# Silu on ScalarE, the last layer's batch 0 first, and the third attention's additions dealt out: a two-layer transformer of 2 x 128 tokens on one core

## The chip, the cores and the metric

The kernel runs on one core of one Trainium2 chip, in one launch. The metric is the device time of that launch in microseconds (us). The engines are PE (TensorE), DVE (VectorE), ACT (ScalarE), POOL (GpSimd) and SP, which issues most DMAs; each takes its own instructions in order and waits for the others by semaphores.

## What the reference computes

Six residual blocks run one after the other over `x`, 2 batches of 128 tokens by 128 channels, each on a layer norm of `x`:

```python
x = x + cross_attention(ln(x), ctx)        # A: causal, so only the first tile of the context counts
x = x + self_attention_with_rope(ln(x))    # B: causal
x = x + top2_of_8_experts(ln(x))           # C: routing, capacity 20, relu MLP
x = x + masked_cross_attention(ln(x), ctx, mask)   # D
x = x + gated_scan(ln(x))                  # E
x = x + bitlinear_mlp(ln(x))               # F
```

What the change touches, cut to what matters:

```python
probs = softmax(x @ Wr + br); topk_p, topk_e = top_k(probs, 2)             # C
scores = where(keep, scores, -inf); out = softmax(scores) @ v              # D
u = silu(conv(u)); b, c = split(u @ W_bc + b_bc)                           # E
state = state * a + b;  y = state * c * sigmoid(gate);  y @ W_out + b_out  # E
gate = silu(bitlinear(x, w_gate)); up = bitlinear(x, w_up)                 # F
return bitlinear(gate * up, w_down)      # F: rounds its input with a scale from each row's greatest |value|
```

## The kernel before, in words

Tokens lie on the 128 partitions, and the two batches are separate tiles. The order of the work is written out by hand: one program for each engine, with semaphores between them, so that an instruction that waits holds up all that stands behind it on its engine. PSUM's eight banks have fixed uses: `S` is banks 0 to 3, `T` 4 and 5, `O` 6 and `D` 7, and `bank(half, g)` is the same memory seen by halves. `keep_warm(name)` (L1036) is a row of `WARM[name]` PE products of constants that nobody reads. A float32 product on PE is two passes in the trace (x2 for one `mm`).

**C, routing** (L1256 to L1281 on PE, L753 to L798 on DVE). PE makes the logits and adds their bias `br` with a product of one row (K=1). DVE takes the greatest, ACT the exponential, and DVE goes through a chain of small operations: the top 2, one-hot rows (`oh1`, `ohb`, `oh`), the softmax's sum and quotient (`lsum`, `lmax`, `prob`, `gates`), and from PE's count of earlier tokens the places and the dispatch matrix `disp` (L790). PE gathers the tokens with it (`C_buf`), ACT copies both batches to `buf` (L452), PE turns the combine matrix `comb` (L1279) and starts the experts' first layer (L1285, four groups `i`). In code `link` makes DVE wait for the end of an instruction; instructions without it follow each other closely.

**D, the third attention** (PE from L1415, DVE from L910, ACT L492). Two context tiles per batch and 16 heads make four *pairs* q = 0 to 3 (two for each batch), each of four banks i. For each pair PE puts the mask's bias and the scores into four banks, DVE takes the maxima (`greatest_of_pair`, R), joins and scales them (RJ, MQ, EX), PE turns RJ between (`turn_maxima_of_pair`) and subtracts EX from the scores (`subtract_of_pair`), ACT takes the exponential of one bank after the other into PX (L495), and PE adds up (`add_up(q, i)`: 8 products, 4 for the sums and 4 for the weighted values, 16 passes in the trace). Both pairs of a batch add to one region (`sums_and_outputs`), which a product sets to zero first. DVE then divides (`divided_by_sums`, RC and AT), PE projects (`project_pairs`), and DVE adds to X and starts the next layer norm. Pair 2 takes its scores into the banks that pair 0 left, pair 3 those of pair 1, except its bank 0.

**E, the scan** (PE from L1478, DVE from L935, ACT L502). PE makes u and the gate from xnT with `win`; half 1 of u's convolution runs on PE (`taps`, 4 products), half 0 on DVE (`conv`, L938 to L945). ACT takes tanh(u/2) (L507, L509) and DVE makes `su` = u (1 + tanh(u/2)), which is 2 silu(u) (L949). PE makes b and c from su (16 passes), DVE adds b's bias and halves it (`bT`, L957), scans (L961), applies the gate (L966) and c with its bias (L971), and PE makes the output (`wout`), whose bias row is multiplied by 4 (`fours`, L1505).

**F, the last layer** (PE from L1515, DVE from L987, ACT L517). For each batch DVE rounds the normed tokens to integers (xq), PE turns them, ACT copies them (xqT) and PE makes gate and up. PE turns both batches before the first gate product (L1516 to L1523). ACT takes the tanh (L523), and DVE makes the product in two instructions (L1006, L1008), the greatest of each row and the scale (L1010 to L1012). ACT scales and rounds both batches (L526), DVE finishes both (hq, L1015), PE turns hq and multiplies with the down weights, and DVE adds to X (L1022), which SP stores.

The core of F on DVE before:

```python
for b in range(B):
    e.wait_ge(sem("F_th"), b + 1)
    link(e.scalar_tensor_tensor(hm[:, b, :], thf[:, b, :], 1.0, S[:, 2 * b, :], ALU.add, ALU.mult))        # L1006
    link(e.scalar_tensor_tensor(hm[:, b, :], hm[:, b, :], kk[:, b:b + 1], S[:, 2 * b + 1, :], ...))        # L1008
    link(e.tensor_reduce(hmax[:, b:b + 1], hm[:, b, :], AX.X, ALU.max, apply_absolute_value=True))         # L1010
    ...
```

Of the kernel before, what the change touches and what calls it, by code (L numbers as in the profile page):

```python
# [13 lines left out]
P = 128  # L14
B = 2
# [12 lines left out]
WARM = dict(A_greatest=5, A_second=4, C_route=9, C_place=3, F_wait=18, B_keys=3, B_queries=3, C_first=2, C_second=3, C_third=0, D_greatest=8, D_second=3,  start=17, A_q=4, A_norm=4, B_norm=7, C_norm=7, D_norm=5, E_conv=4, E_gate=2, E_norm=9)  # L28
# [20 lines left out]
ROWS, ROWS_W = columns(bv=P, bo=P, br=E, bproj=P, bout=P, cb=P)  # L49
# [6 lines left out]
def program(nc, d):  # L56
    with ExitStack() as ctx:
# [51 lines left out]
        fours = sb("fours", [1, P])  # L109
# [98 lines left out]
        th = sb("th", [P, 2, B * P])  # L208
# [3 lines left out]
        bT = sb("bT", [P, 2, B * P])  # L212
# [4 lines left out]
        bbc2 = sb("bbc2", [P, 2])  # L217
# [43 lines left out]
        def pair_bank(q, i):  # L261

            return bank(0, 0) if q == 3 and i == 0 else bank(q % 2, i)

        def spare_of(q):

            return (bank(1, 0)[:, 0:P], bank(0, 0)[:, 0:P], bank(1, 1)[:, 0:P], bank(1, 0)[:, 2 * P:3 * P])[q]

        def sums_and_outputs(b):

            region = (bank(1, 0), bank(0, 1))[b]
            return region[:, 0:P], region[:, P:2 * P]
# [50 lines left out]
        def _(e):  # L323
            e.memset(neghalf[:, :], -0.5).then_inc(sem("pool_const"), 1)
            e.memset(ones[:, :], 1.0).then_inc(sem("pool_const"), 1)
            e.memset(fours[:, :], 4.0).then_inc(sem("pool_const"), 1)
# [34 lines left out]
            e.tensor_scalar(bbc2[:, :], part(scanw, SCAN, "bbc")[:, 2:4], 2.0, None, ALU.mult).then_inc(sem("scan_const"), 1)  # L361
# [25 lines left out]
        def _(e):  # L387
# [62 lines left out]
            for b in range(B):  # L450
                e.wait_ge(sem("C_buf"), b + 1)
                e.activation(buf[:, :, b, :], T[:, b, 0:E * SLOTS].rearrange("p (e s) -> p e s", e=E),  # L452
                             ACT.Copy).then_inc(sem("C_bufs"), 1)
# [38 lines left out]
            for q in range(2 * B):  # L492
                for i in range(G):
                    e.wait_ge(sem("pair_shifted"), G * q + i + 1)
# [12 lines left out]
            e.activation(th[:, 1, :], O[:, 0:B * P], ACT.Tanh, scale=0.5).then_inc(sem("E_th"), 1)  # L507
            e.wait_ge(sem("E_conv"), 1)
            e.activation(th[:, 0, :], conv[:, :, :].rearrange("p b t -> p (b t)"), ACT.Tanh,  # L509
                         scale=0.5).then_inc(sem("E_th"), 1)  # L510
# [9 lines left out]
            for b in range(B):  # L520
# [1110 lines left out]
```

## Time and profile before

| what | value |
|---|---|
| time, median of 3 runs | 142.76 us (142.53 to 145.39) |
| time of the profiled execution | 142.53 us |
| its span, first to last instruction | 140.40 us |
| around the span | 2.13 us |
| busy: PE, DVE, ACT, POOL | 118.4, 85.7, 38.3, 31.5 us |
| chain that ended last | PE 64%, DVE 25%, ACT 6%, issue 3%, POOL 1% |
| mean granted PE clock | 0.979 of full speed |

The times in the rows are microseconds from the span's start, so a row's start plus its length can be set against the next row's start. The chain of waits is followed back from the last instruction: a piece in it ended last among what the next piece waited for. A busy PE isn't a PE on that chain, since the keep-warm products count as busy. The ends of products are modelled: in a row of passes the distance between starts is the cost of one, and the last one's length comes on top.

### The profile page before, as it was taken

Reading aid. Unit: us, or ns where it says so; the run is one execution under the profiler, and the core shown is the slowest. Engines: PE = TensorE matmul, PEld = TensorE weight load, DVE = VectorE, ACT = ScalarE, POOL = GpSimd, SP = SyncE. Lnnn points to the kernel's source line nnn. Section 1 sums busy time; section 2 is a strip of 40 time slices with the busy share of each in tenths; the row PEclk is TensorE's granted clock in tenths of the full one; section 3 lists DMA queues with packets and bytes.
Section 4 is the critical chain, followed back from the end, with each engine's and each line's share of the span. In section 5 each row is a group of like instructions: output and inputs, shape, how many; then the busy total and the mean of one; then the engine's idle time right before and its main releaser. Section 6 shows DMA issues by size and latency. Waiting matters only on the chain.

```text
span 140.4 us, 2885 instructions
## 1 busy us (share of the span) xinstructions
PE 118.4 (84%) x1189; PEld 70.1 (50%) x1189; DVE 85.7 (61%) x227; ACT 38.3 (27%) x88; POOL 31.5 (22%) x53
## 2 busy tenths in 40 slices
PE   6999776986798699789999998789997989983932
PEld 2464223761425365459995542355475467741411
DVE  0635867666958354595325578575746425977872
ACT  3140052400141522137330300551414034002340
POOL 8930000011000011000001199999401100030000
PEclk9999999999999999999999999999999779999996
DMA  3989993010000000000000000000000000000001
GB/s 131 375 296 424 430 421 138 25 51 9 0 0 5 0 0 0 5 0 0 0 5 0 0 7 0 0 0 5 0 7 5 0 5 0 0 0 0 2 0 37
DMA packets 3225, 8.35 MB, mean 60 GB/s; under 512 B 357, under 2 KB 1673, under 8 KB 2954
## 3 DMA queue, kind: packets, MB, share of 16 engines
q1 hardware_dynamic: 3066, 7.72, 14.4%
q10 hardware_dynamic: 144, 0.43, 0.9%
q8 instruction: 10, 0.16, 0.5%
q14 instruction: 5, 0.04, 0.1%
HBM read 8.02 MB, written 0.13 MB: 58 GB/s over the span
## 4 chain that ended last, share of the span: by engine, by line
PE 64%; DVE 25%; ACT 6%; issue 3%; POOL 1%; DVEq 0%; POOLq 0%
PE banks L1029 35%; DVE R L581 5%; PE banks L1403 5%; PE banks L1046 3%; PE banks L1373 3%; PE banks L1061 3%; ACT PX L495 3%; PE banks L1305 3%; PE banks L1387 3%; DVE R L882 2%; PE banks L1069 2%; PE banks L1079 2%; PE banks L1034 1%; PE banks L1365 1%; ACT PX L397 1%
## 5 line engine op out<-in xcount | busy, mean ns | idle before, releaser
L1029 PE MATMUL banks<-onesb 128*128 128x512 bf16 x123 | 32.5, 403 | 2.7 <-POOL onesb L327 1.3
L344 POOL TENSOR_TENSOR rstd<-veps,neghalf 128x1 f32<-128x1 f32 x12 | 6.6, 552 | 91.1 <-DVE veps L563 91.1
L1029 PEld LDWEIGHTS banks<-onesb 128*128 128x128 bf16 x123 | 11.7, 102 | 18.6 <-issue 6.5
L397 ACT ACTIVATE PX<-banks 128x512 f32<-128x512 f32 x16 | 8.3, 603 | 18.6 <-PE banks L1046 18.6
L495 ACT ACTIVATE PX<-banks 128x512 f32<-128x512 f32 x16 | 8.3, 602 | 17.8 <-PE banks L1387 17.8
L581 DVE TRANSPOSE_TENSOR_REDUCE R<-banks 128x32 f32<-128x1024 f32 x8 | 9.5, 1227 | 3.6 <-PE banks L1061 3.6
L882 DVE TRANSPOSE_TENSOR_REDUCE R<-banks 128x64 f32<-128x2048 f32 (+2 forms) x6 | 9.5, 1597 | 3.2 <-PE banks L1373 3.2
L412 ACT ACTIVATE xnT<-banks 128x128 f32<-128x128 f32 x10 | 2.7, 280 | 20.5 <-PE banks L1034 20.5
L1029 PE MATMUL banks<-buf,w 128*128 128x64 f32 x64 | 7.3, 276 | 0.0
L1029 PEld LDWEIGHTS banks<-buf,w 128*128 128x128 f32 x64 | 7.2, 192 | 0.1
L568 DVE TENSOR_SCALAR xn<-X,mv,rstd 128x128 f32<-128x128 f32 x12 | 4.1, 344 | 4.8 <-POOL rstd L344 4.8
L1403 PE MATMUL banks<-PX,oneg 128*32 128x128 f32 x128 | 6.6, 279 | 0.0
L557 DVE TENSOR_TENSOR X<-X,banks 128x128 f32<-128x128 f32 x8 | 2.3, 286 | 7.1 <-PE banks L1029 7.1
L561 DVE BATCH_NORM_STATS2 stats<-X 128x6 f32<-128x128 f32 x12 | 3.5, 294 | 4.8 <-DMA X<-in_x 4.4
L1403 PE MATMUL banks<-PX,VX 128*32 128x128 f32 x128 | 6.4, 273 | 0.0
L1373 PE MATMUL banks<-QS,KT 32*128 32x512 f32 x32 | 6.2, 587 | 0.0
L1046 PE MATMUL banks<-EX,ones 32*128 32x512 f32 x32 | 5.0, 636 | 1.2 <-DVE EX L591 1.1
L1029 PE MATMUL banks<-constb 128*128 128x512 bf16 x16 | 4.8, 382 | 1.4 <-DVE QT L713 0.9
L1069 PE MATMUL banks<-PX,oneg 128*32 128x128 f32 x128 | 4.9, 278 | 1.2 <-ACT PX L397 1.2
L373 POOL TENSOR_SCALAR wtmp<-wtmp 128x512 f32<-128x512 f32 x3 | 5.8, 1935 | 0.3
L1061 PE MATMUL banks<-QB,KT 32*128 32x512 f32 x32 | 5.4, 630 | 0.3 <-DVE QB L574 0.3
L1387 PE MATMUL banks<-EX,ones 32*128 32x512 f32 x32 | 5.2, 613 | 0.0
(222 smaller groups left out, 206.9 us busy)
## 6 DMA issues: line engine op xcount, KB each, us to landing
w<-in_w SPq DMA_DIRECT2D x4, 512.0 KB, 7.5
w<-in_w SPq DMA_DIRECT2D x2, 1024.0 KB, 11.5
scanw<-in_scanw SPq DMA_DIRECT2D x1, 906.0 KB, 13.8
ffn<-in_ffn SPq DMA_DIRECT2D x1, 768.0 KB, 15.0
const<-in_const ACTq DMA_DIRECT2D x1, 417.5 KB, 3.5
selfw<-in_selfw SPq DMA_DIRECT2D x1, 384.0 KB, 3.7
first<-in_first SPq DMA_DIRECT2D x1, 321.0 KB, 4.2
cross<-in_cross SPq DMA_DIRECT2D x1, 320.0 KB, 4.1
```

Source lines behind the costliest of these rows:

```text
L344: e.tensor_tensor(rstd[:, b:b + 1], veps[:, b:b + 1], neghalf[:, 0:1], ALU.pow).then_inc(sem("rstd"), 1)
L397: e.activation(PX[:, u, g, :], bank(half, g), ACT.Exp).then_inc(sem(f"ex{u}"), 1)
L495: e.activation(PX[:, q, i, :], pair_bank(q, i), ACT.Exp).then_inc(sem("pair_exp"), 1)
L581: e.tensor_reduce(R[:, b, 2 * k:2 * k + 2, 0:J * G], banks[:, 4 * b + 2 * k:4 * b + 2 * k + 2, :].rearrange("p g (c i) -> p g c i", i=32), ...
L882: step(e.tensor_reduce(R[:, q % 2, first:first + n, 0:J * G], source.rearrange("p g (c i) -> p g c i", i=32), AX.X, ALU.max, negate=True, ...
L1029: return e.matmul(out, lhsT, rhs, start=start, stop=stop, skip_group_check=True)
L1046: e.matmul(bank(half, g), quarter(ones, g)[:, :], quarter(EX, g)[:, b, :, :].rearrange("p j k -> p (j k)"), start=False, stop=True, tile_p ...
L1061: e.matmul(bank(b, g), quarter(KT, g)[:, b, :], quarter(QB, g)[:, b, :, :].rearrange("p j k -> p (j k)"), start=False, stop=False, tile_po ...
L1069: last = e.matmul(bank(b, 1)[32 * j:32 * j + 32, 0:P], oneg[:, 32 * g:32 * g + 32], PX[:, b, g, j * P:(j + 1) * P], start=(g == 0), stop=( ...
L1373: e.matmul(pair_bank(q, i), quarter(KT, i)[:, q, :], quarter(QS, i)[:, q, :, :].rearrange("p j k -> p (j k)"), start=False, stop=False, ti ...
L1387: e.matmul(pair_bank(q, i), quarter(ones, i)[:, :], quarter(EX, i)[:, q % 2, :, :].rearrange("p j k -> p (j k)"), start=False, stop=True, ...
L1403: last = e.matmul(region[32 * j:32 * j + 32, :], w, PX[:, q, i, j * P:(j + 1) * P], start=False, stop=end, tile_position=(0, 32 * j), skip ...
```

## The change

It does the following (of PE's part of D the diff shows the calls without their waits):

- **Routing (C)**: both bias products of the logits stand ahead of the two batches' products. The softmax's sum, reciprocal, quotient and gates move from among the one-hot operations to behind the dispatch. Batch 1's `buf` is copied by DVE. PE turns `comb` after the first group of the experts' first layer.
- **Third attention (D)**: the additions stand one at a time where PE waited, in the order below. Pair 2 too takes its bank 0 apart (its maximum in two instructions), bank 0 of pairs 2 and 3 comes last in subtraction, exponential and addition, the sums have other banks, and the zeroing is one bf16 product. The row `D_second` (3) goes, `D_divide` (3, ahead of the last projection) comes, `D_norm` is 7 for 5. DVE normalises batch 0 (L926) after batch 1's division.
- **Scan (E)**: ACT takes Silu in place of Tanh, with one Silu of a single column after the last exponential. DVE's `su` and `bT` operations go; b's bias comes by four K=1 products on PE, ahead of `E_conv`, which is 1 for 4. The gate keeps its Tanh.
- **Last layer (F)**: PE turns batch 0 and makes its gate and up products before it turns batch 1. ACT takes Silu, DVE's product is one instruction; ACT rounds batch 0, DVE batch 1. `F_wait` is 12 for 18.

```diff
-WARM = dict(... F_wait=18, ... D_greatest=8, D_second=3, ... D_norm=5, E_conv=4, ...)
+WARM = dict(... F_wait=12, ... D_greatest=8, ... D_norm=7, D_divide=3, E_conv=1, ...)
...
         def pair_bank(q, i):
-            return bank(0, 0) if q == 3 and i == 0 else bank(q % 2, i)
+            if i == 0 and q > 1:
+                return (bank(1, 0), bank(0, 1))[q - 2]
+            return bank(q % 2, i)
+        def unit_order(q):
+            return (0, 1, 2, 3) if q < 2 else (1, 2, 3, 0)
...
# ACT
+            e.activation(tabled[:, :], part(scanw, SCAN, "ld")[:, 0:1], ACT.Silu)
...
-            e.activation(th[:, 1, :], O[:, 0:B * P], ACT.Tanh, scale=0.5).then_inc(sem("E_th"), 1)
+            e.activation(su[:, 1, :], O[:, 0:B * P], ACT.Silu).then_inc(sem("E_su"), 1)
...
                 e.activation(tile(xqT, b), T[:, b, :].bitcast(BF16)[:, 0:P], ACT.Copy).then_inc(sem("F_xqs"), 1)
-            for b in range(B):
                 e.wait_ge(sem("F_gate"), 2 * b + 1)
                 e.wait_ge(sem("F_ch"), b + 1)
-                e.activation(thf[:, b, :], S[:, 2 * b, :], ACT.Tanh, scale=ch[:, b:b + 1]).then_inc(sem("F_th"), 1)
+                e.activation(thf[:, b, :], S[:, 2 * b, :], ACT.Silu, scale=ch[:, b:b + 1]).then_inc(sem("F_th"), 1)
...
# DVE, routing: after disp
+            link(e.tensor_reduce(lsum[:, :], lg[:, :, :], AX.X, ALU.add))
+            link(e.reciprocal(lmax[:, :], lsum[:, :]))
+            e.wait_ge(sem("C_buf"), 2)
+            e.tensor_copy(buf[:, :, 1, :], T[:, 1, 0:E * SLOTS].rearrange("p (e s) -> p e s", e=E)).then_inc(sem("C_bufs"), 1)
+            link(e.tensor_tensor(prob[:, :, :], lg[:, :, :], lmax[:, :].unsqueeze(2).to_broadcast([P, B, E]), ALU.mult))
+            link(e.tensor_tensor(gates[:, :, :], oh[:, :, :], prob[:, :, :], ALU.mult))
...
# DVE, third attention
-            greatest_of_pair(2, 12, 0, 4)
+            greatest_of_pair(2, 11, 1, 3)
+            greatest_of_pair(2, 12, 0, 1)
...
             first_batch("D_")
-            normalise(4, 0)
             divided_by_sums(1)
...
+            normalise(4, 0)
             residual("D_", 1)
...
# DVE, last layer
-            link(e.tensor_tensor(kk[:, :], ch[:, :], fx[:, :], ALU.mult))
-            link(e.tensor_scalar(kk[:, :], kk[:, :], wmean[:, 1:2], None, ALU.mult))
+            link(e.tensor_scalar(kk[:, :], fx[:, :], wmean[:, 1:2], None, ALU.mult))
+            def product(b):
+                e.wait_ge(sem("F_th"), b + 1)
+                e.wait_ge(sem("F_gate"), 2 * b + 2)
+                link(e.scalar_tensor_tensor(hm[:, b, :], thf[:, b, :], kk[:, b:b + 1], S[:, 2 * b + 1, :], ALU.mult, ALU.mult))
+            def rounded(b):
+                e.tensor_scalar(hq[:, b, :], thf[:, b, :], MAGIC, 127.0, ALU.subtract, ALU.min).then_inc(sem("F_hq"), 1)
+            product(0)
+            peak(hm[:, 0, :], hmax[:, 0:1], kd[:, 0:1], sh[:, 0:1], "F_sh")
+            product(1)
+            e.wait_ge(sem("F_round"), 1)
+            rounded(0)
+            peak(hm[:, 1, :], hmax[:, 1:2], kd[:, 1:2], sh[:, 1:2])
+            link(e.tensor_scalar(thf[:, 1, :], hm[:, 1, :], sh[:, 1:2], MAGIC, ALU.mult, ALU.add))
+            rounded(1)
...
# PE, third attention, from pair 0's exponentials on
+            add_up(0, 0)
             turn_maxima_of_pair(1)
+            add_up(0, 1)
-            bias_of_pair(2, range(G))
-            scores_of_pair(2, range(G))
+            bias_of_pair(2, (1, 2, 3))
+            scores_of_pair(2, (1, 2, 3))
             subtract_of_pair(1)
-            for i in range(G):
-                add_up(0, i)
+            add_up(0, 2)
+            bias_of_pair(2, (0,))
+            scores_of_pair(2, (0,))
+            add_up(0, 3)
+            add_up(1, 0)
             turn_maxima_of_pair(2)
-            for i in range(2):
-                add_up(1, i)
+            add_up(1, 1)
             bias_of_pair(3, (1, 2, 3))
             scores_of_pair(3, (1, 2, 3))
             subtract_of_pair(2)
+            add_up(1, 2)
             bias_of_pair(3, (0,))
             scores_of_pair(3, (0,))
-            for i in range(2, G):
-                add_up(1, i)
+            add_up(1, 3)
             turn_maxima_of_pair(3)
-            for i in range(G):
-                add_up(2, i)
+            add_up(2, 1)
             subtract_of_pair(3)
+            add_up(2, 2)
+            add_up(2, 3)
             project_pairs(0)
-            for i in range(G):
-                add_up(3, i)
+            add_up(2, 0)
+            for k, i in enumerate(unit_order(3)):
+                add_up(3, i)
+            keep_warm("D_divide", bank(0, 0))
...
# PE, scan
+            for ct in range(2):
+                for b in range(B):
+                    mm(T[:, ct, b * P:(b + 1) * P], part(rows, ROWS, "bb")[:, ct * P:(ct + 1) * P], ones[0:1, :],
+                       start=(b == 0), stop=False)
             keep_warm("E_conv", D)
```

## Rows read from the trace of the kernel before

**Rows 1.** The chain of waits: start us, us, what.

```profile
59.57 0.08 DVE prob L775
...
93.18 1.89 PE banks L1403 x64
...
114.55 9.09 PE banks L1029 x44
```

**Rows 2.** The windows: us, busy by engine (instructions), PEclk, DMA share, GB/s.

```profile
112.00:114.00 2.00, 1.63 (x5) 1.15 (x4) 0.00 (x0) 0.34 (x2) 0.00 (x0) 0.50 0.00 0
...
124.00:127.30 3.30, 1.86 (x10) 0.67 (x8) 2.95 (x15) 0.00 (x0) 1.13 (x2) 1.00 0.00 0
```

**Rows 3.** The timeline of stage C: start, length, instruction [idle before].

```profile
56.70 0.38 PE L1029 MATMUL banks<-rows,ones 1*128 1x8 f32 x2
...
60.46 0.76 DVE L790 TENSOR_TENSOR disp<-place,const 128x256 f32<-128x256 f32 x2
...
61.67 0.82 ACT L452 ACTIVATE buf<-banks 128x256 f32<-128x256 f32 x2 [3.83 <-PE banks L1029]
...
62.07 0.66 PE L1279 MATMUL banks<-const,comb 128*128 128x128 f32 x4
...
62.56 7.34 PE L1029 MATMUL banks<-buf,w 128*128 128x64 f32 x64
```

**Rows 4.** The timeline of stage D, pair 3 and the last division.

```profile
98.78 1.02 PE L1373 MATMUL banks<-QS,KT 32*128 32x512 f32 x2
...
101.56 0.69 DVE L898 TENSOR_TENSOR EX<-MQ,const 128x512 f32<-128x512 f32 x1
...
103.63 1.14 PE L1387 MATMUL banks<-EX,ones 32*128 32x512 f32 x8
...
104.60 0.38 PE L1029 MATMUL banks<-rows,ones 1*128 1x128 f32 x2
...
104.79 2.07 ACT L495 ACTIVATE PX<-banks 128x512 f32<-128x512 f32 x4 [4.81 <-PE banks L1387]
...
107.62 0.96 DVE L906 RECIPROCAL RC<-banks 128x128 f32<-128x128 f32 x1
```

**Rows 5.** The timeline from the norm ahead of E to E's output.

```profile
111.89 0.42 PE L1034 MATMUL banks<-const,xn 128*128 128x128 f32 x1
...
112.68 1.79 PE L1029 MATMUL banks<-xnT,scanw 128*128 128x256 f32 x4 [0.37 <-ACT xnT L412]
...
116.36 1.02 PE L1029 MATMUL banks<-xnT,scanw 128*128 128x256 f32 x4
...
117.22 1.03 PE L1029 MATMUL banks<-onesb 128*128 128x512 bf16 x4
...
117.47 0.42 DVE L949 SCALAR_TENSOR_TENSOR su<-th,conv 128x256 f32<-128x256 f32 x1
...
122.06 0.71 PE L1029 MATMUL banks<-rows,fours 1*128 1x128 f32 x4
```

**Rows 6.** The timeline of stage F, from the last small operation before the products.

```profile
129.20 0.23 DVE L1003 TENSOR_SCALAR kk<-kk,wmean 128x2 f32<-128x2 f32 x1
129.41 1.26 ACT L523 ACTIVATE PX<-banks,ch 128x512 f32<-128x512 f32 x2
...
130.20 0.69 DVE L1006 SCALAR_TENSOR_TENSOR PX<-PX,banks 128x512 f32<-128x512 f32 x1 [0.77 <-ACT PX L523]
130.92 0.75 DVE L1008 SCALAR_TENSOR_TENSOR PX<-PX,kk,banks 128x512 f32<-128x512 f32 x1
131.71 0.69 DVE L1010 TENSOR_REDUCE hmax<-PX 128x1 f32<-128x512 f32 x1
...
135.29 0.81 ACT L526 ACTIVATE PX<-PX,magic,sh 128x512 f32<-128x512 f32 x1 [1.66 <-DVE sh L1012]
...
136.13 0.43 DVE L1015 TENSOR_SCALAR hq<-PX 128x512 bf16<-128x512 f32 x1 [0.56 <-ACT PX L526]
```

**Rows 7.** The timeline of ACT at the kernel's start.

```profile
1.15 1.28 ACT L391 ACT_TABLE_LOAD   x1 [1.15 <-PEq L1623]
```

More of the change, by code:

```diff
@@ L26 @@
 NEG = -1e30
-WARM = dict(A_greatest=5, A_second=4, C_route=9, C_place=3, F_wait=18, B_keys=3, B_queries=3, C_first=2, C_second=3, C_third=0, D_greatest=8, D_second=3,  start=17, A_q=4, A_norm=4, B_norm=7, C_norm=7, D_norm=5, E_conv=4, E_gate=2, E_norm=9)
+WARM = dict(A_greatest=5, A_second=4, C_route=9, C_place=3, F_wait=12, B_keys=3, B_queries=3, C_first=2, C_second=3, C_third=0, D_greatest=8,  start=17, A_q=4, A_norm=4, B_norm=7, C_norm=7, D_norm=7, D_divide=3, E_conv=1, E_gate=2, E_norm=9)
 ZEROED = 12
@@ L765, in _ @@
             link(last)
-            e.tensor_copy(topf[:, :, :], topi[:, :, 0:2])
-            link(e.tensor_reduce(lsum[:, :], lg[:, :, :], AX.X, ALU.add))
+            link(e.tensor_copy(topf[:, :, :], topi[:, :, 0:2]))
             ex = part(const, CONST, "expert")
             for b in range(B):
-                e.tensor_scalar(oh1[:, b, :], ex, topf[:, b, 0:1], None, ALU.is_equal)
-            link(e.reciprocal(lmax[:, :], lsum[:, :]))
+                last = e.tensor_scalar(oh1[:, b, :], ex, topf[:, b, 0:1], None, ALU.is_equal)
+            link(last)
             for b in range(B):
@@ L778, in _ @@
             link(last)
-            e.tensor_scalar(far[:, :, :], oh[:, :, :], 1.0, -2.0 * P, ALU.subtract, ALU.mult)
-            link(e.tensor_tensor(gates[:, :, :], oh[:, :, :], prob[:, :, :], ALU.mult))
+            link(e.tensor_scalar(far[:, :, :], oh[:, :, :], 1.0, -2.0 * P, ALU.subtract, ALU.mult))
             e.wait_ge(sem("C_cnt"), 1)
@@ L1257, in _ @@
             for b in range(B):
+                mm(S[:, 2, b * E:(b + 1) * E], ones[0:1, :], part(rows, ROWS, "br"), start=(b == 0), stop=False)
+            for b in range(B):
                 if b:
@@ L1261, in _ @@
                 e.wait_ge(sem("xnT"), 2 * B + b + 1)
-                mm(S[:, 2, b * E:(b + 1) * E], tile(xnT, b), part(moe, MOE, "wr"), stop=False)
-                last = mm(S[:, 2, b * E:(b + 1) * E], ones[0:1, :], part(rows, ROWS, "br"), start=False)
+                last = mm(S[:, 2, b * E:(b + 1) * E], tile(xnT, b), part(moe, MOE, "wr"), start=False)
             last.then_inc(sem("C_logits"), 1)
@@ L1274, in _ @@
                     .then_inc(sem("C_buf"), 1)
-            e.wait_ge(sem("C_comb"), B)
-            for b in range(B):
-                for h in range(2):
-                    q = 2 * b + h
-                    last = e.transpose(D[:, q * P:(q + 1) * P],
-                                       comb[:, b * E + 4 * h:b * E + 4 * h + 4, :].rearrange("p e s -> p (e s)"), ident)
-            last.then_inc(sem("C_ct"), 1)
             e.wait_ge(sem("C_bufs"), 2)
@@ L1291, in _ @@
                 last.then_inc(sem("C_hp"), 1)
+                if i == 0:
+                    e.wait_ge(sem("C_comb"), B)
+                    for b in range(B):
+                        for h in range(2):
+                            q = 2 * b + h
+                            last = e.transpose(D[:, q * P:(q + 1) * P],
+                                               comb[:, b * E + 4 * h:b * E + 4 * h + 4, :].rearrange("p e s -> p (e s)"), ident)
+                    last.then_inc(sem("C_ct"), 1)
             e.wait_ge(sem("D_mask"), B * NS)
@@ L1504, in _ @@
             for b in range(B):
-                mm(S[:, b, 0:P], fours[0:1, :], part(rows, ROWS, "bout"), stop=False)
+                mm(S[:, b, 0:P], twos[0:1, :], part(rows, ROWS, "bout"), stop=False)
             for kt in range(2):
```

116 lines of the change are left out of this document (48 added, 68 removed).

## The prediction

> **What bounds the kernel now.** I read the chain of waits first, then the timeline of each stage that the change touches, then the windows for PE's clock. The chain changes its engine by stage, so each stage needs its own sum. In routing it is DVE, in operations that cost 0.08 us each where the next doesn't wait for them. In the third attention it is PE: four additions (64 passes) take 1.89 us with the last one's tail, some 0.43 us each without. From 114.55 on it is PE alone for 9.09 us, the whole of E's products [rows 1]. In F it is DVE, from the product to the last rounding [rows 6]. Between D and E there is a stretch in which PE was granted half its clock (0.50) [rows 2]. The sum is made against the profiled execution: 142.53 us, a span of 140.40 and 2.13 around it. The median shown is 0.23 above it, which I leave to the range.
>
> **Routing: -0.1.** The bias row of the logits ended PE's part; its two passes begin at 56.70, and the bias ahead of the products takes some 0.3 off, less a little where one more such pair delays the norm's transposition: -0.25. Four operations of 0.08 leave the chain (`lsum`, `lmax`, `prob`, and `gates` beside `far`): -0.33 [rows 1, 3]. So `disp`, now at 60.46, comes at 59.9. Behind it PE gathers; ACT copied both batches from 61.67 to 62.49 while PE turned `comb` from 62.07, and the experts began at 62.56 [rows 3]. Now DVE's copy of batch 1 (0.42, by `su` as the nearest DVE row of 128x256 [rows 5]) ends near 62.0, and the experts begin there, 0.55 earlier. But the four turns, which were hidden under the copies, now stand between two groups of the experts with nothing to hide them: 4 x 0.11 = 0.45 on PE. Net -0.1. What moves behind `disp` delays DVE's first bias addition and ACT's first relu, and both have caught up by the second group. Bounds: -0.55 (the turns cost nothing) to +0.3 (DVE's copy waits for the links ahead of it).
>
> **Third attention: -0.5.** The additions are the same 16; what counts is PE's idle time that they fill. Pair 2's bank 0 now comes apart, which adds a pass pair of 1.02, as long for one bank as for four [rows 4], and a second maximum; in exchange the turn of pair 2 no longer queues behind four additions. I take these as even, so EX of pair 3 still ends at 101.56 + 0.69 = 102.25. There the gain lies: the subtraction waited behind additions until 103.63 and now starts at once, 1.4 earlier. PE then has: the subtraction until the next work could start, 104.60 - 103.63 = 0.97; the projection, two pairs of passes at some 0.3; seven additions (three of pair 2, four of pair 3) at 0.43, 3.0. That is 102.25 + 4.6 + 0.25 for the tail = 107.1, where the division started at 107.62: -0.5 [rows 1, 4]. The exponentials don't hold it: the first comes 1.16 after the subtraction starts, as before, and the four end 2.07 later, at 105.5, ahead of their additions [rows 4]. So of 1.4 only 0.5 is kept, as PE has the additions left over. Batch 0's normalisation moved behind the division fits into DVE's wait for the projection. Bounds: -1.4 (all kept) to +0.5 (the split costs half a scores pair more than it frees).
>
> **The clock: -0.9.** The four `win` passes take 1.79 in the half-clock stretch and 1.02 for the same four shapes at full clock: 0.77 [rows 5]. The transposition ahead of them takes 0.42 there, some 0.12 more than at full clock, and it queued behind keep-warm products at half speed, another 0.2; against that, ACT's copy will end last, 0.2 later than the passes. Now `D_divide` fills part of PE's pause before the last projection, and `D_norm` has two more. I take it that the stretch stays at 2.4 GHz: -0.9. A pause of PE by itself doesn't settle it: from 124.0 to 127.3 it is busy 1.86 of 3.30 and is granted 1.00 [rows 2]. Bounds: -1.1 to +0.4, the latter with the half clock and two keep-warm products more.
>
> **Scan: +0.5.** PE is the whole chain here [rows 1], and the four `E_conv` products ran right up to the first product of su [rows 5]. Three go: 3 x 0.214 = -0.64. The b bias brings 4 products of one row, 8 passes; the `fours` products show 0.71 for four of the kind, so 0.71 + 4 x 0.11 = 1.15 [rows 5]. Net +0.5. That `su` (0.42) and `bT` go from DVE gives nothing: behind them PE was, and stays, the last to arrive. Bounds: +0.8 (a gap at each change of row groups) to -0.5 (bias passes hidden, and su's 0.42 gained).
>
> **Last layer: -2.2.** Batch 0's gate product no longer waits for batch 1's turn, so its Silu (taken as long as the tanh, 0.68, at 129.41 before) is over when DVE comes from batch 1's `kk`. Of the two `kk` operations one goes, so the product starts at 129.2 instead of 130.20: -1.0 [rows 6]. From there, step to step: product 0.78, greatest 0.72, scale and reciprocal 0.27, batch 1's product 0.78, a wait for ACT's rounding 0.2, batch 0's hq 0.42, greatest 0.70, scale and reciprocal 0.38, DVE's own scaling and rounding 0.5 (nearest row hq's 0.43, and 0.75 at most), which is 4.75: hq of batch 1 at 133.95 instead of 136.13 [rows 6]. ACT's 0.81 for batch 1 is gone and so are two operations of 0.69. Behind hq all stays. `F_wait`, 12 at 0.214, ends ahead of batch 1's turn. Bounds: -2.5 to -1.6 (DVE's scaling at 0.75, and the second Silu late by 0.4).
>
> **ACT's table: 0.** No row shows Silu. A table load is 1.28 us of ACT [rows 7]; the single-column Silu draws it into the time between the last exponential (105.5) and the next copy (behind the division, which starts at 107.1), so it is hidden; with that cover gone it costs up to 1.3. The gate's Tanh comes between two uses of Silu. The Trainium skill (ScalarE: Activation LUTs, "Table sets: the hidden batching unit") says that functions are loaded in sets and that each change of set is another load; it lists tanh with exp's set and with sigmoid's, and doesn't list silu's. By its figure of about 2.66 us for a switch with its drain the first one would still be hidden; the trace shows the 1.28 and not the drain.
>
> **Sum.** -0.1 - 0.5 - 0.9 + 0.5 - 2.2 = -3.2: 142.53 - 3.2 = **139.3 us**.
>
> **Rivals.** (1) The half-clock stretch stays. For it: the pause between the sums and the projection is only partly filled, by 3 products. Against: 10 keep-warm products where there were 5. Then the 0.9 is missing, and two more at half clock add 0.4: 140.6. (2) E isn't held by PE: bias passes run under other waits, and DVE's 0.42 counts. For it: no row shows eight such passes in a row. Against: 9.09 us of unbroken PE [rows 1]. 139.3 - 0.5 - 0.5 = 138.3. (3) Tanh and Silu exclude each other, so ACT loads twice more. The load for the gate is hidden under the products of b; the last one, if it stands behind the wait for the gate product, delays both products by 1.1: 140.4. For it: tanh and exp needed one load between them in all the trace. Against: at the start the load ran at 1.15, ahead of its instruction's wait [rows 7], and ACT idles there. This is the skill's rule of the paragraph on the table, acting here. (4) The dealing out doesn't shorten D: the extra pass pair and maximum of pair 2 lie on the chain and take what the earlier subtraction gives; D at +0.5: 140.3. (5) Slower than before: PE is granted half its clock in E. Where the granted clock falls may shift once all moves by 1 to 3 us; products there are dense, and at half clock 2 us do the work of 1. It decides from 3.2 us lost: two stretches of 2 us like the one of rows 2 lose 1.0 each, with the missing 0.9 no more than 2.9; four of them, nearly all of E, lose 4.9 in all: 144.2. For it: the clock did fall once in this trace, right ahead of E [rows 2]. Against: E is PE's densest part.
>
> **Chances.** Forecast 0.55, with its own range 138.7 to 139.9; (1) 0.12, (2) 0.10, (3) 0.08, (4) 0.10, (5) 0.05. A measurement of this kernel tells about 2% from no change, which is below 139.9 or above 145.6. Faster by more: nine tenths of the forecast, (2), and 0.03 where two terms of the others meet, 0.63. Slower by more: 0.03, part of (5). Within 2%: 0.34. The range takes in (1), (3), (4) and nearly (2), 138.3 to 140.8, which leaves out (5) and the ends of the bounds.
>
> **What would show it.** Routing: experts' first product some 0.55 earlier, but the turns among them. D: the last subtraction right behind its EX, and PE without a gap from there to the last sums. Clock: 1.00 in all windows between D and E, `win` passes near 1.0. E: DVE waiting for PE, 1.1 us of one-row passes ahead of the products of su. F: product of batch 0 right after `kk`, no ACT rounding for batch 1. One ACT_TABLE_LOAD more, in the gap after the last exponential. I am wrong if the clock in D to F falls elsewhere, if more loads show, or if E's products of su start right behind ACT's Silu rather than behind PE's own rows.

## The result and the profile after

The changed kernel took 140.45 us (median of 4 runs, 140.35 to 140.56) beside 142.53 to 145.59 for the kernel before on the same chip: a ratio of 0.985, interval 0.982 to 0.987. The forecast was 139.3, so the time fell by 1.5% where 2.3% was forecast. The profiled execution took 140.56 us with a span of 138.6, against 142.53 and 140.40: the span fell by 1.80 us where 3.2 were forecast. How long an execution takes also depends on where PE is granted half its clock in it; the ratios leave out the executions that lost most by it, and below, stages are compared where both stood at full clock, or the text says so.

The span can be cut at six points that both traces have. The start of one instruction to the start of the next named one:

| stretch | before | after | change | forecast |
|---|---|---|---|---|
| start to D's first mask bias | 80.50 | 80.39 | -0.11 | -0.1 |
| to the last division (RC) | 27.12 | 27.61 | +0.49 | -0.5 |
| to the convolution's products (`taps`) | 6.93 | 6.09 | -0.84 | -0.9 |
| to the first product of su | 3.53 | 4.07 | +0.54 | +0.5 |
| to batch 0's addition to X | 5.59 | 5.59 | 0 | 0 |
| to hq of batch 1 | 12.46 | 10.61 | -1.85 | -2.2 |
| to the end | 4.27 | 4.24 | -0.03 | 0 |

Of the forecast's terms (the five of its sum and the table's 0), routing, clock, scan and ACT's table came within 0.1. D has the wrong sign, and F is 0.35 short.

**Routing.** The timeline of stage C in the profile of after, to be set beside [rows 3]:

```profile
59.84 0.76 DVE L785 TENSOR_TENSOR disp<-place,const 128x256 f32<-128x256 f32 x2
...
61.56 0.42 DVE L791 COPY buf<-banks 128x256 f32<-128x256 f32 x1 [0.68 <-PE banks L1028]
...
62.04 2.00 PE L1028 MATMUL banks<-buf,w 128*128 128x64 f32 x16 [0.59 <-DVE buf L791]
...
63.87 0.61 PE L1290 MATMUL banks<-const,comb 128*128 128x128 f32 x4
```

`disp` comes 0.62 earlier, the experts 0.52 earlier, released by DVE's copy, and the four turns stand between the first and the second group, 0.45 to the next product. So nearly all of the 0.52 is spent again.

**Third attention.** Its timeline of DVE and POOL around the first EX, and from the last EX on (compare [rows 4]):

```profile
83.12 2.35 POOL L366 TENSOR_SCALAR taps<-const,scanw 128x128 f32<-128x128 f32 x4
84.33 0.40 DVE L890 TENSOR_TENSOR RJ<-R 128x64 f32<-128x64 f32 x1
85.45 0.70 POOL L374 TENSOR_SCALAR wtmp<-ffn,wscale 128x512 f32<-128x512 f32 x1
85.48 1.20 DVE L898 TENSOR_TENSOR EX<-MQ,const 128x512 f32<-128x512 f32 x1
...
101.89 0.69 DVE L898 TENSOR_TENSOR EX<-MQ,const 128x512 f32<-128x512 f32 x1
102.63 1.14 PE L1388 MATMUL banks<-EX,ones 32*128 32x512 f32 x8 [0.32 <-DVE EX L898]
103.70 0.43 PE L1405 MATMUL banks<-PX,oneg 128*32 128x128 f32 x8
104.72 0.48 PE L1028 MATMUL banks<-rows,ones 1*128 1x128 f32 x2
105.55 0.43 PE L1405 MATMUL banks<-PX,oneg 128*32 128x128 f32 x8
...
105.87 1.28 ACT L501 ACT_TABLE_LOAD   x1
...
107.17 0.20 ACT L501 ACTIVATE tabled<-scanw 128x1 f32<-128x1 f32 x1
...
108.00 0.96 DVE L906 RECIPROCAL RC<-banks 128x128 f32<-128x128 f32 x1 [1.33 <-PE banks L1405]
```

The subtraction starts right behind the last EX, as forecast: at 102.63 where it was 103.63. But the first EX took 1.20 where it took 0.69 before, and it started 0.03 behind an operation of POOL that before came 0.34 after it. The kernel before met POOL at another place, pair 2's EX, which took 1.00:

```profile
85.41 0.69 DVE L898 TENSOR_TENSOR EX<-MQ,const 128x512 f32<-128x512 f32 x1
85.75 0.91 POOL L371 TENSOR_SCALAR wtmp<-ffn,wscale 128x512 f32<-128x512 f32 x1
...
95.69 1.00 DVE L898 TENSOR_TENSOR EX<-MQ,const 128x512 f32<-128x512 f32 x1
```

The first of these rows and the one of 1.20 belong to pair 0, ahead of the reordered work in D. From the end of the last EX to RC pass 5.42 us, with PE at work all the way, where 4.85 were forecast. The table load is the one that was forecast, hidden; no other appears behind it.

**Clock, scan.** The windows, to be set beside [rows 2], and the timeline up to the products of su, beside [rows 5]:

```profile
112.00:114.00 2.00, 1.49 (x7) 0.81 (x5) 0.00 (x0) 0.81 (x3) 0.00 (x0) 1.00 0.00 0
```

```profile
112.09 0.27 PE L1033 MATMUL banks<-const,xn 128*128 128x128 f32 x1
112.73 1.13 PE L1028 MATMUL banks<-xnT,scanw 128*128 128x256 f32 x4 [0.37 <-ACT xnT L415]
...
116.42 0.42 ACT L512 ACTIVATE su<-conv 128x256 f32<-128x256 f32 x1
116.74 0.82 ACT L516 ACTIVATE thg<-banks,bgh 128x256 f32<-128x256 f32 x2
116.85 1.15 PE L1028 MATMUL banks<-ones,rows 1*128 1x128 f32 x8
117.93 0.39 PE L1028 MATMUL banks<-onesb 128*128 128x512 bf16 x1
118.16 3.62 PE L1028 MATMUL banks<-su,scanw 128*128 128x256 f32 x16
```

The granted clock is 1.00 where it was 0.50, the transposition takes 0.27 for 0.42 and the four `win` passes 1.13 for 1.79. In the scan, su is ready at 116.84 and isn't used before 118.16: PE is still at the eight one-row passes of b's bias (116.85 to 117.93) and the one keep-warm product. The gate's Tanh (116.74) follows the Silu without a table load.

**Last layer.** Its timeline from the first product, beside [rows 6], and the one piece of its chain of waits that has no counterpart before:

```profile
129.21 0.75 DVE L1000 SCALAR_TENSOR_TENSOR PX<-PX,kk,banks 128x512 f32<-128x512 f32 x1
...
130.99 0.75 DVE L1000 SCALAR_TENSOR_TENSOR PX<-PX,kk,banks 128x512 f32<-128x512 f32 x1
131.09 0.81 ACT L526 ACTIVATE PX<-PX,magic,sh 128x512 f32<-128x512 f32 x1 [0.41 <-DVE sh L981]
132.40 0.43 DVE L1005 TENSOR_SCALAR hq<-PX 128x512 bf16<-128x512 f32 x1 [0.67 <-ACT PX L526]
...
134.36 0.43 DVE L1005 TENSOR_SCALAR hq<-PX 128x512 bf16<-128x512 f32 x1
```

```profile
131.94 0.02 DVEq L1010
131.97 0.43 issue
132.40 0.43 DVE hq L1005
```

The product starts at 129.21 (forecast 129.2). ACT's rounding ends at 131.90, yet DVE's hq of batch 0 starts only at 132.40; for 0.43 us of that the chain shows no releaser at all ("issue").

### The profile page after: what moved, and what is told of

The parts are those of the page before. It is cut to its first block, busy times and chain, and to the rows that moved or that the text cites. A ratio compares the mean times of both kernels' runs of the same rounds, so it can differ in the third digit from the quotient of the medians.

```text
span 138.6 us, 2879 instructions
## 1 busy us (share of the span) xinstructions
PE 117.9 (85%) x1188; PEld 69.0 (50%) x1188; DVE 84.1 (61%) x223; ACT 38.5 (28%) x88; POOL 31.9 (23%) x52
## 4 chain that ended last, share of the span: by engine, by line
PE 66%; DVE 24%; ACT 4%; issue 3%; POOL 1%; DVEq 0%; POOLq 0%
PE banks L1028 37%; DVE R L581 5%; PE banks L1405 4%; PE banks L1374 4%; PE banks L1045 3%; PE banks L1388 3%; PE banks L1060 3%; DVE R L882 3%; PE banks L1306 3%; PE banks L1068 2%; PE banks L1078 2%; PE banks L1366 2%; PE banks L1033 1%; ACT PX L400 1%; DVE EX L591 1%
## 5 line engine op out<-in xcount | busy, mean ns | idle before, releaser
L1028 PE MATMUL banks<-onesb 128*128 128x512 bf16 x116 | 30.2, 397 | 2.0 <-POOL onesb L331 1.3
L1028 PEld LDWEIGHTS banks<-onesb 128*128 128x128 bf16 x116 | 11.1, 103 | 16.4 <-issue 6.3
L882 DVE TRANSPOSE_TENSOR_REDUCE R<-banks 128x48 f32<-128x1536 f32 (+2 forms) x7 | 9.7, 1393 | 3.9 <-PE banks L1374 3.9
L1374 PE MATMUL banks<-QS,KT 32*128 32x512 f32 x32 | 7.2, 587 | 0.0
L1045 PE MATMUL banks<-EX,ones 32*128 32x512 f32 x32 | 5.0, 636 | 1.2 <-DVE EX L591 1.1
L1405 PEld LDWEIGHTS banks<-PX,oneg 128*32 128x32 f32 x128 | 3.0, 108 | 4.4 <-issue 3.8
```

What stands on the lines that cost most here:

```text
L882: step(e.tensor_reduce(R[:, q % 2, first:first + n, 0:J * G], source.rearrange("p g (c i) -> p g c i", i=32), AX.X, ALU.max, negate=True, ...
L1028: return e.matmul(out, lhsT, rhs, start=start, stop=stop, skip_group_check=True)
L1045: e.matmul(bank(half, g), quarter(ones, g)[:, :], quarter(EX, g)[:, b, :, :].rearrange("p j k -> p (j k)"), start=False, stop=True, tile_p ...
L1374: e.matmul(pair_bank(q, i), quarter(KT, i)[:, q, :], quarter(QS, i)[:, q, :, :].rearrange("p j k -> p (j k)"), start=False, stop=False, ti ...
L1405: last = e.matmul(region[32 * j:32 * j + 32, :], w, PX[:, q, i, j * P:(j + 1) * P], start=False, stop=end, tile_position=(0, 32 * j), skip ...
```

## The experiments

Four claims are tested here: DVE loses 0.47 us in D to POOL; the dealing out by itself neither gains nor loses (before run 1 it was held to lose the 0.5 itself); the scan's loss is the eight one-row passes; the 0.43 us in F isn't a wait for ACT. Runs shared a chip with runs of the kernel before in each batch.

**1. The third attention's order undone.** Banks, zeroing, order, maxima and the row `D_second` of D as before, all else as changed:

```diff
-            greatest_of_pair(2, 11, 1, 3)
-            greatest_of_pair(2, 12, 0, 1)
+            greatest_of_pair(2, 12, 0, 4)
...
-            add_up(2, 1)
+            for i in range(G):
+                e.wait_ge(sem("pair_exp"), 2 * G + max(i + 1, 2))
+                add_up(2, i)
             subtract_of_pair(3)
...
-            add_up(2, 2)
-            add_up(2, 3)
             project_pairs(0)
```

> The changed kernel with the third attention's order, banks and zeroing as before (D_divide and D_norm stay as changed). Theory: the dealing out itself lost time, since taking pair 2's bank 0 apart adds a pass pair, a maximum and a wait for an exponential to the chain; then the last division starts at about 107.5 instead of 108.0 and the time is 140.0. Rival: the order is worth what I forecast and something outside it (the slower EX operations beside POOL's work) cost 1 us; then undoing it loses the gain as well and the time is 140.9 or more.

D took 27.12 us again (first bias 81.15, RC 108.27), 0.49 less than in the changed kernel, with the stretch behind the division and the scan as changed (6.08 and 4.07). The profiled time, 140.52, is no lower than the changed kernel's, as the stages ahead of D took 0.76 us longer in this execution (first bias at 81.15 for 80.39). The run doesn't show that the order carries the +0.49. Pair 0's operations, which lie ahead of all that the edit moves, differ too:

```profile
85.09 0.22 DVE L884 TENSOR_TENSOR RJ<-R 128x64 f32<-128x64 f32 x1
...
86.06 0.69 DVE L892 TENSOR_TENSOR EX<-MQ,const 128x512 f32<-128x512 f32 x1
86.26 1.05 POOL L368 TENSOR_SCALAR wtmp<-ffn,wscale 128x512 f32<-128x512 f32 x1
```

RJ and the first EX came through undisturbed here. The last EX ends 21.74 behind the first bias for 22.19, and RC follows 5.38 later for 5.42, so 0.45 of the 0.49 lies ahead of the last EX's end, where the order and the meeting with POOL can't be told apart by this run. Runs 3, 7 and 11, which keep the dealt-out order, end the last EX at 21.72, 21.88 and 21.72, so most of the 0.45 is POOL's.

**2. Only the keep-warm rows.** The kernel before with `D_divide` = 3 and `D_norm` = 7:

> The kernel before with only the three D_divide products added and D_norm at 7. Theory: the half-clock stretch ahead of E goes and gives 0.8 to 0.9: 141.7, with a granted clock of 1.00 from 108 to 116. Rival: the clock came back because the rest moved, so the stretch stays and the two more products at half clock make it 0.4 slower: 142.9.

From RC (108.72) to `taps` (114.80) it took 6.08 us, for 6.93 before. Its windows:

```profile
112.00:114.00 2.00, 1.63 (x9) 0.88 (x8) 0.35 (x1) 0.28 (x1) 0.29 (x1) 1.00 0.00 0
...
131.00:133.00 2.00, 2.00 (x6) 0.63 (x5) 1.86 (x6) 0.00 (x0) 0.00 (x0) 0.50 0.01 4
```

So the five products alone give the 0.85 in this execution, and in all thirteen profiles that have them the clock is 1.00 in this stretch, which takes 6.08 or 6.09. The four best times are 141.58 to 141.88, beside 142.33 to 142.57 for the kernel before. The ratio is 0.995 (0.990 to 0.9996): the half clock now fell in the last layer, where PE isn't what the others wait for, and F took 12.46 as before.

**3. POOL's work on the last layer's weights held back** until the last EX and cut to one operation for each matrix (it leaves out their scaling and rounding):

```diff
+            e.wait_ge(sem("pair_ready"), 4)
...
-                e.tensor_scalar(wtmp[:, :], w, wscale[:, m:m + 1], MAGIC, ALU.mult, ALU.add).then_inc(sem("w_round"), 1)
...
+                e.tensor_scalar(wq3[:, m, :], w, -1.0, None, ALU.max).then_inc(sem("w_round"), 3)
```

> The changed kernel with POOL's preparation of the last layer's weights held back until the last EX is made, and cut to one operation per matrix (the weights are neither scaled nor rounded, which this leaves out). Theory: EX of pairs 0 and 2 took 1.20 and 1.06 us because POOL worked beside DVE; with POOL still all four take 0.69, and the last division starts 0.4 to 0.6 earlier: 139.9 to 140.1. Rival: the slower EX is hidden by PE's additions, and the time stays at 140.4 although EX is 0.69.

All four EX took 0.69, the last from 102.25 on, which is 21.72 us from the first bias (81.22) to its end; the changed kernel took 22.19, the kernel before 21.75. That is the 0.47. RJ took 0.23 here although `taps` wasn't held back, so its share, 0.18 by runs 9 and 10, isn't the edit's doing; the EX make up the rest. It leaves the dealt-out order even with the kernel before, with pair 2's bank taken apart, its extra pass pair and its maximum; but the kernel before had its own EX of 1.00, so this isn't yet a comparison of the two orders undisturbed (see run 9). The best times were 139.92 to 139.96 (ratio 0.979, 0.974 to 0.985). In the profile the clock fell to 0.50 at 102 to 105, so what came behind EX isn't read from it.

**4. b's bias back on DVE.** Four products fewer on PE, two `bT` operations on DVE:

```diff
-                    mm(T[:, ct, b * P:(b + 1) * P], part(rows, ROWS, "bb")[:, ct * P:(ct + 1) * P], ones[0:1, :],
-                       start=(b == 0), stop=False)
...
+                return step(e.tensor_scalar(bT[:, ct, :], T[:, ct, 0:B * P], bbc[:, ct:ct + 1], None, ALU.add))
```

> The changed kernel with b's bias back on DVE (one addition per half ahead of each scan) and without the eight one-row passes on PE. Theory: the passes were on PE's chain, and without them the products of su start behind ACT's Silu at some 117.0 instead of 118.16; DVE's two more operations stay in its slack: 139.3 to 139.4. Rival: DVE's chain (0.5 per bias) becomes the last to arrive at the output products, and no more than 0.5 is gained: 139.9 or more.

PE's timeline from the convolution on, at full clock:

```profile
118.92 1.97 PE L1035 MATMUL banks<-upad,taps 128*128 128x256 f32 x8 [0.23 <-ACT upad L508]
120.72 1.02 PE L1035 MATMUL banks<-xnT,scanw 128*128 128x256 f32 x4
121.58 0.38 PE L1035 MATMUL banks<-onesb 128*128 128x512 bf16 x1
121.80 1.48 PE L1035 MATMUL banks<-su,scanw 128*128 128x256 f32 x6
```

2.88 us from `taps` to su's product instead of 4.07, and from there to X 5.61 (5.59 before): DVE's two operations cost nothing. The profiled execution was 143.97, with half clock in D; the best time is 139.01, the ratio 0.977 (0.968 to 0.986).

**5. The changed kernel again**, in a later batch:

> The changed kernel once more, unchanged, beside the other runs of this chip. Theory (where the granted clock falls, and whether it does, differs between executions, not between these kernels): the stages at full clock keep their lengths of before within 0.05 us (third attention 27.6 from its first bias to the last reciprocal, 6.1 from there to the convolution's products, 4.07 to the first product of su, 8.65 from batch 0's addition to X in the scan to batch 0's hq), and the times lie between 140.0 and 141.0, with a stage up to 3 us longer where the clock falls in it. Rival (the changed kernel by its own timing holds the clock at full speed all through): the clock is 1.00 in every window from 54 to 137 again, as in its first profile.

D 27.54, then 6.08, 4.07, and 8.65 to batch 0's hq: the stages repeat within 0.07. The times don't: 140.34 with a mean granted clock of 0.997, then 141.72, 141.83, 142.72 and 145.66 with 0.984 down to 0.951; the ratio is 0.992 (0.987 to 0.996). In this profile the clock was 0.50 from 129 to 136. The rival is out: the change doesn't hold the clock by itself, and the first four runs, all at 0.997, make the gain look larger than it is on average.

**6. Two copies of one column on DVE**, in its wait for the scan's output:

```diff
+            for k in range(2):
+                e.tensor_copy(lmax[:, k:k + 1], lsum[:, k:k + 1])
```

> The changed kernel with two copies of one column more on DVE, in its wait for the scan's output (nobody reads what they write). They do nothing but move all later instructions of DVE in its stream. Theory (the 0.4 us in which DVE stood before batch 0's second rounding belongs to the place in the stream of instructions, as two kernels with other counts of DVE instructions do not show it): from batch 0's addition to X to its hq 8.3 us in place of 8.65, and the time 0.3 to 0.4 lower. Rival (it belongs to the wait for ACT's rounding, or it is the chip's): 8.65 again and the time unchanged.

The chain of waits of this run in F:

```profile
135.77 0.04 DVE sh L983
135.80 0.43 issue
136.24 0.76 DVE PX L1002
...
137.02 0.43 DVE hq L1007
```

The same 0.43 us now stands ahead of batch 1's product, and hq follows without a gap. X to hq took 8.40, not the 8.3 expected: 0.13 more than the 8.27 of run 1, as batch 1's product now ends 0.2 behind ACT's rounding. The best times were 140.07 to 140.09 against 140.34. So it isn't the wait for ACT: it sits at a place in DVE's stream. The kernels with b's two operations on DVE and the dealt-out order (runs 4 and 10), which shift the stream as much, show 8.40 too; those with the old order of D, which has another count, 8.27 or 8.28. The trace of DMA has a companion to the pause: one transfer of the kind `instruction` (8 KB) starts 0.65 us behind its end in the changed kernel (133.05), 0.67 in this run (136.91), and 0.65 to 0.67 in all nine profiles that show the pause. That ties it to the loading of instructions, but doesn't show that the load causes it, which stays open.

**7. One addition more ahead of the last turn**, another ahead of the last subtraction:

```diff
+            e.wait_ge(sem("pair_exp"), 2 * G + 2)
+            add_up(2, 1)
             e.wait_ge(sem("pair_exp"), 2 * G + 3)
             turn_maxima_of_pair(3)
-            add_up(2, 1)
+            add_up(2, 2)
             subtract_of_pair(3)
...
-            add_up(2, 2)
             add_up(2, 3)
```

> The changed kernel with one addition of pair 2 more ahead of the last turn and the other ahead of the last subtraction, so that PE has two additions behind the last subtraction less one. Theory (the third attention ends by the work that PE has left behind the last subtraction: seven additions and the projection): PE had 0.74 us without work ahead of the last turn and 0.5 ahead of the last subtraction, an addition takes 0.43, so the last reciprocal starts 0.3 to 0.45 us earlier, 27.2 from the first bias in place of 27.6, and the time falls by as much. Rival (the last exponentials or DVE's chain of the maximum hold the end, and PE's queue only fills behind them): 27.6 again, or longer by 0.4 because the turn and the subtraction come behind the additions.

D took 27.18, 0.43 less, but for another reason than expected: in this execution no EX was disturbed (all 0.69), though POOL's work and all of pair 0 are as in the changed kernel. That is worth 0.47. From the last EX's end to RC it took 5.30 instead of 5.42, as the five additions behind the projection took 2.67 here instead of 2.37, for a reason that the trace doesn't show. The time is 140.26 at best. This run alone settles nothing on the filling; run 10 does.

**8. Old order of D and b on DVE** (edits 1 and 4 together):

> The changed kernel with the third attention in the order of before (its keep-warm rows as changed, and the row of three behind the second maxima back) and with the scan's b bias on DVE, as before the change. Theory (these two parts of the change lose 0.49 and 1.19 us, independently of each other): 27.1 from the first bias to the last reciprocal, 2.9 from the convolution's products to the first product of su, and 140.45 - 0.49 - 1.19 = 138.8, or 138.4 without the 0.4 of DVE ahead of batch 0's second rounding. Rival (what is gained early is given back behind it, in the last layer or to the clock): not below 139.5.

27.14 and 2.88. The best three times are 138.58, 138.76 and 138.81 (ratio 0.977, 0.973 to 0.982): the two parts add up as expected.

**9. POOL's nine operations put between the EX** by waits, nothing left out; the same with the old order and b on DVE, and with the filling and b on DVE:

```diff
+                e.wait_ge(sem("pair_ready"), m + 1)
                 e.tensor_scalar(wtmp[:, :], w, wscale[:, m:m + 1], MAGIC, ALU.mult, ALU.add).then_inc(sem("w_round"), 1)
...
                 e.wait_ge(sem("w_round"), 3 * m + 2)
+                e.wait_ge(sem("pair_ready"), m + 2)
```

> The changed kernel with POOL's nine operations on the last layer's weights put between the four EX of DVE by waits for them; nothing is left out. Theory (an EX beside one of those operations takes 1.0 to 1.2 us in place of 0.69, and that, not the order of the additions, makes the last EX of the changed kernel end 0.47 late; the order itself neither gains nor loses): all four EX 0.69, 21.7 from the first bias to the end of the last EX and 27.1 to the last reciprocal (27.6 without, 27.1 before the change). Rival (the dealt-out order gains the 0.5 that was forecast once EX is undisturbed): 26.6 to the last reciprocal.

All EX 0.69, but PE had half its clock for ten microseconds of D in the profile, so its length can't be read; the best times are 140.13 and 140.32, hardly under the changed kernel's. Inconclusive on the 0.47.

> The third attention in the order of before, b's bias on DVE, POOL's operations put between the EX, the rest as changed. Theory (the order of before had one EX beside POOL too, 1.02 for 0.69): 26.8 from the first bias to the last reciprocal in place of 27.1, and 138.3 us where the same without the last edit took 138.6 to 138.8. Rival (POOL's later end delays the next norm's power or the last layer's products, or the 0.3 falls into a wait of PE): 27.1 and not below 138.6.

27.08 where 26.8 was expected: the third EX fell to 0.69, but pair 0's RJ took 0.40 beside POOL's `taps` in this execution and cost 0.18. Even so the last EX ends 21.70 behind the first bias. Without the 0.18 it would be 21.5, an estimate, where the dealt-out order undisturbed has 21.72 (run 3): so the split of pair 2's bank does seem to cost some 0.2, which the kernel before hid by losing as much to POOL. The best time is 138.54, no gain that can be measured.

**10.** The filled order with the same edit:

> The dealt-out order with two additions moved ahead into PE's idle time, b's bias on DVE, POOL's operations put between the EX. Theory (undisturbed, the two orders end within 0.2 of each other, as PE's work behind the last subtraction sets the end and the idle time that can be filled ahead of it is small): 26.9 from the first bias to the last reciprocal, 138.4 us, within 0.2 of the kernel with the order of before. Rival (the filling gives a whole addition more than the order of before): 26.4 and 137.9.

The chain of waits behind the last EX:

```profile
103.04 0.70 DVE EX L901
...
103.78 1.14 PE banks L1397 x8
104.92 0.58 PE banks L1414 x16
105.50 0.83 PE banks L1037 x4
106.33 2.37 PE banks L1414 x80
...
108.72 0.97 DVE RC L909
```

One addition (16 passes) ahead of the projection instead of two, and 4.99 us from EX to RC: exactly 0.43 less than 5.42, as PE's work alone would have it. The last EX ends 22.07 behind the first bias: 21.72, 0.18 for RJ beside POOL again, and 0.17 because the turn now queues behind an addition. D is 27.06, and the best times are 138.63 and 138.76. Both orders, with every EX at 0.69 and RJ at 0.40, end within 0.02 of each other (27.08 in run 9), the dealt-out one with the help of the filling.

**11. One POOL instruction more.** The change had dropped an operation of two columns with b's bias; it is put back, unread:

```diff
+            e.tensor_scalar(bbc2[:, :], part(scanw, SCAN, "bbc")[:, 2:4], 2.0, None, ALU.mult)
```

> The changed kernel with one operation more: POOL's small operation on two columns (0.21 us) that the change took away with b's bias is put back ahead of the taps, and nobody reads what it writes. Theory (the change lost 0.47 us in the third attention because POOL's later operations came 0.2 us earlier and so started 0.03 us ahead of the first EX instead of behind it): RJ of pair 0 takes 0.23 in place of 0.40 and the first EX 0.69 in place of 1.20, POOL's operation beside it is the longer one; 21.7 from the first bias to the end of the last EX, 27.1 to the last reciprocal in place of 27.6, and the time falls by 0.4 for one instruction more, to 139.9 to 140.1 at best. Rival (the two engines slow each other whichever starts first, or the place of POOL's start has other causes): 1.0 to 1.2 for the first EX and 27.6 again.

The timeline around the first EX, and of pair 2's:

```profile
85.33 0.23 DVE L892 TENSOR_TENSOR RJ<-R 128x64 f32<-128x64 f32 x1
86.30 0.69 DVE L900 TENSOR_TENSOR EX<-MQ,const 128x512 f32<-128x512 f32 x1
86.64 0.91 POOL L376 TENSOR_SCALAR wtmp<-ffn,wscale 128x512 f32<-128x512 f32 x1
...
96.41 0.69 DVE L900 TENSOR_TENSOR EX<-MQ,const 128x512 f32<-128x512 f32 x1
96.43 2.47 POOL L378 TENSOR_SCALAR wtmp<-wtmp 128x512 f32<-128x512 f32 x1
```

POOL's operations are now the long ones (0.91 for 0.70, 2.47 for 1.94), RJ takes 0.23 as before the change, and the last EX ends 21.72 behind the first bias instead of 22.19. The clock fell behind it, so RC isn't read. The best times are 140.07 and 140.11, 0.25 under the changed kernel's 140.34 and less than the 0.4 expected.

## Why the prediction was right or wrong

**Routing, -0.1: right**, for its reason: 0.52 earlier at the experts, 0.45 back for turns that nothing hides.

**Third attention, -0.5: the step that failed.** It measured +0.49, and the 1.0 between has two parts. "EX of pair 3 still ends at 102.25" failed by 0.44 against the first bias: RJ and the first EX ran beside POOL, which no term had; with POOL held back the last EX ends at 21.72 behind that bias, not 22.19 (run 3). "I take these as even" came out, 21.72 against 21.75, but partly by luck: the 21.75 holds an EX of 1.00, and undisturbed the split costs some 0.2 (run 9, an estimate). And the sum behind it, 4.85, was mis-sized by 0.57: the projection takes 0.83, not two times 0.3; two additions to the next work took 1.02, not 0.86; the subtraction 1.07, not 0.97; five additions and their tail 2.45, not 2.40; and 0.05 passes between EX and the subtraction. The 0.83 had a hint in the trace of before: there the projection starts at 104.60 [rows 4] and the next addition at 105.44, though that addition waited for ACT. With 5.42 for 4.85 the earlier subtraction is worth nothing, as measured: 5.37 from EX to RC before.

**Rival (4)** gave the right number for D, +0.5, and 140.3 for the whole, but in the main by another mechanism: the extra passes and maximum took some 0.2 by the estimate of run 9, and POOL and the mis-sized work on PE took the rest.

**Clock, -0.9: right** (-0.84), and run 2 shows that the keep-warm rows do it. Rival (1) is out. That the clock "stays" was right for this stretch only. In other executions of these kernels it falls at 88 to 95, 102 to 109 or 127 to 136, among other places.

**Scan, +0.5: right** (+0.54). The passes took 1.08 to the next start, the sum had 1.15. Rival (2) is out: run 4 gives 1.19 back on PE, and DVE's part costs nothing.

**Last layer, -2.2: right in mechanism, -1.85 in size.** The product started at 129.21 as forecast; from there to hq it took 5.15 for 4.75. The pause of 0.43 in DVE's stream, which run 6 moves, is what is over: run 8, which doesn't show it, took 4.78 from the product to hq, and 10.25 from X to hq where the forecast makes 12.46 - 2.2 = 10.26.

**Table, 0: right.** One load, at 105.87, hidden; rival (3) is out. The single-column Silu begins 0.02 behind the load's end, so the trace shows no separate drain of the kind in the Trainium skill's figure of 2.66 us (ScalarE: Activation LUTs, "What ACT_TABLE_LOAD costs"), only the 1.28.

**Rival (5)**: the clock didn't fall in E in any profile here.

The faster versions found are the changed kernel with b's bias left on DVE, and either order of D: 138.54 to 139.01 at best, a ratio of 0.977 to 0.981 to the kernel before, where the change as made has 0.985 and, repeated, 0.992.

## What to carry to other kernels

An earlier release is worth only what the engine behind it hasn't already got queued: add up that engine's work from the release to the end with durations taken from start to start, and if it fills the stretch, dealing it out differently gains nothing. One-row bias products are cheap only under a wait; on the engine that bounds the stage they cost their full start-to-start time, here 1.1 us for eight passes. When a change moves one engine by 0.2 us, look at what its neighbour on the other engine will now meet. And before a difference between two profiles is put down to an edit, compare the operations ahead of it: where these differ, it is the executions that differ, not only the kernels.

## What had not been expected of the hardware

**DVE beside POOL.** An EX (128x512, two inputs) that starts 0.02 to 0.16 us behind an operation of POOL on the weights takes 1.0 to 1.2 us instead of 0.69; where EX starts first, POOL's operation is the longer one, by 0.2 to 0.5. One in the middle of a POOL operation with bf16 output wasn't lengthened (89.52 beside 88.77 to 90.26 in the trace of before). So the loss turns on some hundredths of a microsecond: at 85.45 against 85.48 DVE lost in the changed kernel, at 96.43 against 96.41 POOL did in run 11. The first EX of the changed kernel came second because RJ, beside `taps`, had taken 0.40, and because POOL was 0.2 ahead. By that 0.2 the change put RJ on an edge. In the three profiles with POOL's two-column operation (before, runs 2 and 11) RJ starts 1.03 us behind the first `taps` and takes 0.23. In the eleven without it, it starts 1.20 behind in five and takes 0.22 or 0.23, and 1.21 to 1.29 behind in six and takes 0.33 to 0.41. So code that is the same up to there loses the 0.47 in one execution and not in another. The Trainium skill (SBUF — State Buffer, "SBUF: two separate sides") says that the two engines share a pair of ports, that it goes to whichever starts first for that whole instruction, and that the other is blocked. Where one of the two was lengthened, who loses agrees with the rows; how much doesn't: the EX at 95.89 started 0.1 behind a POOL operation of 1.94 (95.79) and took 1.06, so it was done long before that operation ended.

**A pause of 0.43 us in DVE's stream** that two one-column copies move by a few instructions, with a transfer of instructions 0.65 us behind its end.

**The granted clock** fell in mid-run in every profile but the changed kernel's first, at several places, and its cost depends on the stage: 0.85 us ahead of E, next to nothing during the first half of F (run 2), and some 4 us in D (run 4: 31.7 from the first bias to RC, for 27.6).
